# Masking attention probabilities by selection, and adding both key tiles on GpSimd before the row sums

## The reference

```
q = _l2norm(q) * q_scale;  k = _l2norm(k) * k_scale          # 16 heads of 64
sim = jnp.einsum('bhid,bhjd->bhij', q, k) * 8.0              # keys: 2 null keys and 256 rows
sim = sim + dist[None, None] * slopes[None, :, None, None]
sim = jnp.where(causal_mask[None, None], neg, sim)
attn = jax.nn.softmax(sim, axis=-1)
out = jnp.einsum('bhij,bhjd->bhid', attn, v)
```

## Time and profile before

| what | value |
|---|---|
| median of three runs | 976.25 us |
| the profiled execution | 976.13 us, of which 974.4 us are the span from first to last instruction |
| PE busy | 926.8 us (95%) |
| PEld, DVE busy | 708.9 us (73%), 736.5 us (76%) |
| ACT, POOL busy | 586.9 us (60%), 592.9 us (61%) |
| granted TensorE clock, mean | 0.989 |

### The profile page before, as it was taken

One profiled execution on the slowest core, in us unless ns is written; L12 is line 12 of the kernel. 1 busy time (PEld: TensorE's weight loads), 2 busy tenths in 40 slices (PEclk: granted clock), 3 DMA queues, 4 the chain that ended last, 5 costly groups with the idle time before them and its releaser, 6 DMA issues.

```text
span 974.4 us, 21588 instructions
## 1 busy us (share of the span) xinstructions
PE 926.8 (95%) x8309; PEld 708.9 (73%) x8309; DVE 736.5 (76%) x2334; ACT 586.9 (60%) x1235; POOL 592.9 (61%) x562
## 2 busy tenths in 40 slices
PE   1887999999999999999999999999999999999996
PEld 1575778687776878677786878668786878768755
DVE  6885578778788697868888787877977668864466
ACT  4448672867467662866648573775738574585622
POOL 5235773677547774677747875577744855458613
PEclk9979899999999999999999999999999999999999
DMA  5400000000000000000000000000000000000000
GB/s 156 109 0 11 2 3 2 0 12 2 13 1 12 1 2 13 1 11 2 13 1 1 12 2 13 1 11 2 12 2 1 1 1 13 1 1 2 13 1 12
DMA packets 22088, 11.50 MB, mean 12 GB/s; under 512 B 7648, under 2 KB 21344, under 8 KB 21856
## 3 DMA queue, kind: packets, MB, share of 16 engines
q1 hardware_dynamic: 20128, 9.51, 3.5%
q10 hardware_dynamic: 1856, 0.59, 0.2%
HBM read 8.00 MB, written 2.10 MB: 10 GB/s over the span
## 4 chain that ended last, share of the span: by engine, by line
PE 82%; DVE 8%; POOL 4%; ACT 4%; issue 1%; DMA 0%; DVEq 0%; ACTq 0%; POOLq 0%
PE bank L1987 8%; PE bank L1704 7%; PE bank L2024 6%; PE bank L1705 6%; PE bank L1706 6%; PE bank L1948 6%; PE bank L1985 5%; PE bank L1711 4%; PE bank L1857 4%; PE bank L1954 3%; PE bank L2120 3%; PE bank L2056 3%; PE bank L2126 3%; PE bank L2057 3%; POOL rnorm L920 3%; PE bank L1912 2%
## 5 line engine op out<-in xcount | busy, mean ns | idle before, releaser
L929 POOL TENSOR_TENSOR square<-square,causal 128x256 f32<-128x256 f32 x128 | 102.0, 821 | 54.4 <-ACT square L1169 54.4
L915 POOL TENSOR_TENSOR rnorm<-sumsq,minus_half 128x16 f32<-128x16 f32 x32 | 93.9, 2937 | 50.0 <-DVE sumsq L1526 49.8
L929 POOL TENSOR_TENSOR unit<-unit,causal 128x256 f32<-128x256 f32 x128 | 92.1, 745 | 38.3 <-ACT unit L1169 38.3
L1948 PE MATMUL bank<-qT,kT 64*128 64x256 f32 x512 | 95.2, 389 | 0.0
L920 POOL TENSOR_TENSOR rnorm<-unit,minus_half 128x32 f32<-128x32 f32 x16 | 91.4, 5720 | 0.0
L1163 ACT ACTIVATE square<-bank,bias_k,rnorm 128x256 f32<-128x256 f32 x128 | 65.7, 570 | 40.8 <-PE bank L1948 40.8
L1954 PE MATMUL bank<-qT,kT 64*128 64x128 f32 x512 | 84.0, 284 | 3.0 <-ACT unit L1169 2.2
L1954 PEld LDWEIGHTS bank<-qT,kT 64*128 64x128 f32 x512 | 71.0, 186 | 17.9 <-ACT unit L1169 6.7
L1948 PEld LDWEIGHTS bank<-qT,kT 64*128 64x128 f32 x512 | 68.7, 186 | 0.7
L1093 ACT ACTIVATE xaT_hi<-bank 128x256 fp32r<-128x256 f32 x16 | 5.5, 382 | 105.5 <-PE bank L1865 105.5
L1163 ACT ACTIVATE unit<-bank,bias_k,rnorm 128x256 f32<-128x256 f32 x96 | 51.4, 574 | 23.2 <-PE bank L1948 23.2
(11 more groups left out here) (402 smaller groups left out, 2905.8 us busy)
## 6 DMA issues: line engine op xcount, KB each, us to landing
xin<-in_L_attn_x SPq DMA_DIRECT2D x7, 256.0 KB, 2.8
out<-x SPq DMA_DIRECT2D x7, 256.0 KB, 2.3
square<-in_L_attn_w_kv SPq DMA_DIRECT2D x1, 1024.0 KB, 6.5
w_sw<-in_L_ffn_sw_w SPq DMA_DIRECT2D x3, 256.0 KB, 7.8
unit<-in_L_attn_w_q SPq DMA_DIRECT2D x1, 512.0 KB, 5.0
w_out<-in_L_attn_w_out SPq DMA_DIRECT2D x8, 64.0 KB, 2.1
w_ml<-in_L_ffn_ml_w SPq DMA_DIRECT2D x2, 256.0 KB, 6.0
xin<-in_L_attn_x ACTq DMA_DIRECT2D x1, 256.0 KB, 3.1
```

The lines of the kernel that those rows point to most:

```text
L915: pool.tensor_tensor(rnorm[:, 1, t, :], sumsq[:, t % 2, :], minus_half[:], ALU.pow).then_inc(a_root.sem, 1)
L929: m = pool.tensor_tensor(pd, pd, causal[:].unsqueeze(1).to_broadcast([P, 2, P]), ALU.mult)
L1948: return mm(bank[s][:, 2 * P * i:2 * P * (i + 1)], kT[rs, p, 2 * P * b:2 * P * b + P], qT[rs, p, 2 * P * b:2 * P * (b + 1)], start=True, s ...
```

## The change

1. Row sums. For the later queries POOL adds the probabilities of both key tiles (`late_sum`, 128x512 a unit, for four heads). PE then streams 128 columns of the sum, where it streamed 128 of key tile 1 and 128 of key tile 0. The weighted values are unchanged. A new semaphore `a_late` tells PE that the sum is there; PE waits for it between the two halves of the row sums.
2. Mask. The multiply by `causal` becomes an `affine_select` that writes zero where the key is later than the query. The six blocks of a pair of heads are laid out anew, so that the four blocks on the diagonal are contiguous: one instruction of 128x512 takes the place of two of 128x256. The tile `causal` and its set-up go.
3. Lists. The lists of all engines change in all stretches.

```diff
+        def early(pr, j):
+            return pr[:, 2 * j::4 - j, :]
+
+        def late(pr, j):
+            return pr[:, 2 * j + 1, :]
...
+        late_probs = []
+        for v in (unit_flat[:, 5 * N:5 * N + 2 * PH], square_flat[:, 0:2 * PH]):
+            blocks = v.rearrange("p (m i q) -> p m i q", m=2, q=P)
+            late_probs.append((blocks[:, :, 4:6, :], blocks[:, :, 1:4:2, :]))
+        late_sum = [hid_sw[1 + i].rearrange("p (m j q) -> p m j q", m=2, q=P) for i in range(2)]
...
                     pool.wait_ge(a_exp.sem, a_exp.at(g, 2 * h + 2))
-                    for b in range(SEQ):
-                        pd = probs[h % 4][:, b, 0::2, :]
-                        m = pool.tensor_tensor(pd, pd, causal[:].unsqueeze(1).to_broadcast([P, 2, P]), ALU.mult)
-                    m.then_inc(a_mask.sem, 1)
+                    pd = probs[h % 4][:, 0:4, :]
+                    pool.affine_select(out=pd, in_=pd, compare_op=ALU.is_ge, fill=0.0, base=0,
+                                       pattern=[[0, 4], [1, P]], channel_multiplier=-1).then_inc(a_mask.sem, 1)
+                pool.wait_ge(a_mask.sem, a_mask.at(g, 2 * c + 2))
+                if c > 1:
+                    pool.wait_ge(a_den.sem, a_den.at(g, c - 1))
+                elif first(g):
+                    pool.wait_ge(all_set, 1)
+                else:
+                    pool.wait_ge(f_e.sem, f_e.at(g - 1))
+                    pool.wait_ge(a_den.sem, a_den.at(g - 1))
+                pool.tensor_tensor(late_sum[c % 2], late_probs[c % 2][0], late_probs[c % 2][1], ALU.add).then_inc(a_late.sem, 1)
...
-                weigh(den, lambda k, h: ones[:]).then_inc(a_den.sem, 1)
+                for rs, h, pr, j in quad:
+                    mm(den[rs, 0:P], ones[:], early(pr, j)[:, 0, :], start=False, stop=True, skip_group_check=True)
+                pe.wait_ge(a_late.sem, a_late.at(g, c + 1))
+                for i, (rs, h, pr, j) in enumerate(quad):
+                    last = mm(den[rs, P:2 * P], ones[:], late_sum[c % 2][:, i % 2, j, :], start=False, stop=True, skip_group_check=True)
+                last.then_inc(a_den.sem, 1)
...
 MIDDLE = {
     "POOL": """
-a_keep f_stats.0 f_stats.1 a_ss.0 f_ce a_ss.1 a_ss.2 f_ce_apply f_ce2 a_ss.3 l_turn2 a_kss.0 l_res f_bias e_stats
+f_stats.0 f_stats.1 a_ss.0 f_ce a_ss.1 f_ce_apply a_ss.2 f_ce2 a_ss.3 l_turn2 l_res f_bias a_kss.0 a_kss.1 a_keep
```

More of the change, by code:

```diff
@@ L59 @@
     "PE": """
[L60 to L63, removed]
+a_m.0 a_m.1 a_k.0 a_null a_k.1 a_t.0 a_m.2 a_kr.0 a_k.2 a_k.3 a_t.1 a_kr.1 a_m.3 a_kt l_turn2 a_v.0 a_t.2 a_v.1
+a_t.3 l_turn3 a_v.2 l_route l_g.0 l_u.0 a_v.3 l_g.1 a_scores.0 l_u.1 l_cT a_nT l_g.2 a_scores.1 l_u.2 a_mix.0 l_c.0
+a_scores.2 a_mix.1 e_turn1 a_scores.3 l_g.3 a_mix.2 l_c.1 a_scores.4 l_u.3 l_g.4 a_mix.3 l_c.2 a_scores.5 a_mix.4
+l_c.3 a_scores.6 l_u.4 a_mix.5 a_scores.7 a_mix.6 l_down.0 l_down.1 a_mix.7 l_down.2 l_down.3 a_out.0 a_out.1 l_x.0
 l_x.1
@@ L549, in program @@
         a_mask = signal("a_mask", H)
+        a_late = signal("a_late", U)
         a_nT = signal("a_nT", 1)
@@ L1159, in score_exps @@
                         if h < STEEP:
-                            act.activation(pr[:, j, 0, :], k0[:, 0, :], ACT.Exp, bias=bias_k0[:, h:h + 1], scale=by)
-                            last = act.activation(pr[:, j, 1, :], k0[:, 1, :], ACT.Exp, bias=bias_k0b[:, h:h + 1], scale=by)
+                            act.activation(early(pr, j)[:, 0, :], k0[:, 0, :], ACT.Exp, bias=bias_k0[:, h:h + 1], scale=by)
+                            last = act.activation(early(pr, j)[:, 1, :], k0[:, 1, :], ACT.Exp, bias=bias_k0b[:, h:h + 1], scale=by)
                         else:
-                            last = act.activation(pr[:, j, 0:2, :], k0, ACT.Exp, bias=bias_k0[:, h:h + 1], scale=by)
+                            last = act.activation(early(pr, j), k0, ACT.Exp, bias=bias_k0[:, h:h + 1], scale=by)
                     last.then_inc(a_exp.sem, 1)
@@ L1168, in score_exps @@
                         by = rnorm[:, 0, 2 * b + 1, h:h + 1]
-                        last = act.activation(pr[:, j, 2, :], bank[2][:, 2 * P * s + P * j:2 * P * s + P * (j + 1)], ACT.Exp,
+                        last = act.activation(late(pr, j), bank[2][:, 2 * P * s + P * j:2 * P * s + P * (j + 1)], ACT.Exp,
                                               bias=bias_k1[:, h:h + 1], scale=by)
@@ L1980, in a_mix_ @@
                 b, q = unit_of(c)
-                quad = [(slice(32 * i, 32 * i + 32), QW * q + i, probs[(2 * c + i % 2) % 4][:, i // 2, :, :]) for i in range(QW)]
+                quad = [(slice(32 * i, 32 * i + 32), QW * q + i, probs[(2 * c + i % 2) % 4], i // 2) for i in range(QW)]
                 def weigh(dst, left):
-                    for rs, h, pr in quad:
-                        mm(dst[rs, P:2 * P], left(1, h), pr[:, 2, :], start=False, stop=False, skip_group_check=True)
-                    for rs, h, pr in quad:
-                        last = mm(dst[rs, :], left(0, h), pr[:, 0:2, :], start=False, stop=True, skip_group_check=True)
+                    for rs, h, pr, j in quad:
+                        mm(dst[rs, P:2 * P], left(1, h), late(pr, j), start=False, stop=False, skip_group_check=True)
+                    for rs, h, pr, j in quad:
+                        last = mm(dst[rs, :], left(0, h), early(pr, j), start=False, stop=True, skip_group_check=True)
                     return last
```

133 lines of the change are left out of this document (65 added, 68 removed).

## The result

| what | before | changed |
|---|---|---|
| median (runs) | 976.12 us (4) | 965.47 us (4; 965.29 to 968.65) |
| ratio to before, 95% interval | | 0.9896 [0.9881, 0.9911] |
| profiled execution, its span | 976.13 us, 974.4 us | 965.40 us, 963.7 us |

A forecast was written before the change was run, and what follows sets the result against it. PE was taken to bound the kernel, busy nearly all of each middle pass. Row sums 13.4 - last attention 1.3 - first attention 0.4 - moved steps 1.8 = 9.9 us; 976.13 - 9.9 = 966.2 us, range 961 to 972.5.

The forecast's parts named there:

- Row sums 0.67 to 0.46 us a unit: PE's row sums as two waves of 128 columns: 0.21 us saved a unit, 64 units, 13.4 us.
- the bound on the last attention: In the last attention ACT's exponentials set 4.55 us a unit, so units 0 to 5 lose their saving: 1.3 us.
- The new wait costs nothing for itself: PE's wait for POOL's sum between the row-sum halves: slack 0.4 us in tight units, so charged nothing.
- Select 0.60, add 1.27 us: POOL's 128x512 instructions: two selects and one add make 2.5 us a unit, 0.4 to 0.8 less than before.
- The bound of 2.6 us from L832: Upper bound for POOL's 128x512 select, if the 0.66 us of a 128x128 select were the rate for four blocks.
- Moved steps, 0.3 us a pass: Root behind the first sum, apply ahead of a_mix.0 delay unit 1's mixing: 1.8 us over five middle passes and the next.
- the 110.1 to 110.5 forecast: Sign of being right: a middle pass 110.1 to 110.5 us long, PE busy for nearly the whole of it.
- On DVE the other steps only change places in time that it has: DVE's list in the middle passes: 22 us idle a pass, so its other reordered steps cost nothing.
- set-up and tail at 0: Changed lists of the set-up and tail: taken as 0, with 1.5 us either way.
- The select may cost 1.0 before a tight unit waits: POOL's select, taken at 0.60 us, could reach 1.0 before PE waits for the sum in tight units; slack 0.4 us.
- The rival in which POOL becomes the bound: Select as slow as L832: sum late from 1.6 us each, 996 us at 2.0 us; chance 0.05.
- The rival of the wait, 972.2 us: The wait between PE's row-sum halves costs 0.1 us a unit, 6.4 us in all; chance 0.15, shared with a slower select.

The follow-up runs named there:

- e5: The kernel before, with a wait for a long-given semaphore (the mask's) between the two waves of its row sums: 976.04 us, ratio 0.9992.
- e11: The changed operations without the add, with the old lists; the late row sums stream the second key tile alone; against the kernel before: 965.26 us, ratio 0.9889.
- e12: The changed kernel (new lists) without the add, the late row sums streaming the second key tile alone: 964.85 us, ratio to the kernel before 0.9882.
- e2: The kernel before, its operations kept, with the changed kernel's work lists: 988.25 us, ratio 1.0127.
- e4: The kernel before with only the mask changed to one select of 128x512 a head pair, no add, old row sums and lists: 975.86 us.
- e10: The changed operations with the old lists and one POOL step moved, f_end_stats ahead of a_scores.5 in the middle passes: 965.95 us, ratio to before 0.9898.
- e3: The changed kernel with e_apply back behind a_mix.0 in DVE's list of the middle passes: 972.61 us, ratio to the kernel before 0.9969.
- e9: The changed kernel with the copy a_keep moved behind e_stats in POOL's list of the middle passes: 967.99 us, ratio to the kernel before 0.9914.
- e6: The changed kernel with each select made twice, a mask costing 1.3 us: 1009.33 us, ratio to the kernel before 1.0323.
- e8: The changed kernel with the mask by multiplication again, the add and short row sums kept: 1021.43 us, ratio to the kernel before 1.0454.

## Why the prediction was right, and where its terms were off

- **Row sums 0.67 to 0.46 us a unit.** Right (0.47 read), and so was the bound on the last attention: two units of eight keep their 0.21 us there, 0.42, and the stretch gave 0.41. The pass behind the middle ones gave 1.67 us = 8 x 0.21, so the 0.3 us that the prediction charged it was wrong.
- **The new wait costs nothing for itself.** Right: no idle time at it in the pass read, and e5 finds a granted wait free.
- **Select 0.60, add 1.27 us.** Right: median 0.64 and 1.27. The bound of 2.6 us from L832 was far off, and the trace of before could have told so. It has a second select of 128x128:

```profile
L794 POOL TENSOR_SCALAR_AFFINE_SELECT ident<-ident x1: 292/292/292, 1.6 to 1.6; 128x128 f32<-128x128 f32 x1
```

  It takes 0.29 us with DVE idle. L832 took 0.66 at 65.86, while DVE's L1304, which reads two tiles in SBUF, ran from 65.15 to 66.37. The figure in the Trainium skill ("GPSIMD Engine Reference", section "3. Performance versus the Vector engine"), 0.77 us for 512 elements by the best software loop, is too slow for this select.
- **Moved steps, 0.3 us a pass.** Right place and chain (root behind the sum, apply ahead of `a_mix.0`, unit 1's mixing), size half of what came: 0.63 us. The working had PE wait 0.1 us and rounded up to 0.3. Of the 0.5 us that this lacks, 0.31 are the apply, taken at 1.11 and measured at 1.42; the root ends 1.00 us behind the start of unit 0's mixing, where 0.73 was worked out. That a pass still came out at 110.33, inside the 110.1 to 110.5 forecast, needs 0.37 us of gain elsewhere (111.75 - 1.68 + 0.63 = 110.70 otherwise). e11 and e12 show that much and more as the gain of PE's new order, a term that the sum put at nothing. So the forecast's closeness is in part luck: two errors of the sum cancel here.
- **"On DVE the other steps only change places in time that it has", set-up and tail at 0.** The tail is right; the set-up can't be told. As a view of the lists it was wrong: alone they lose 12.7 us (e2). The 22 us of idle time a pass said nothing, since the loss comes from one chain that crosses from POOL to DVE.
- **"The select may cost 1.0 before a tight unit waits", and 996 us at 2.0.** This is the step that failed, though the forecast did not rest on it. At 1.3 us the kernel is at 1009 us, already slower than before, at 1.9 us at 1050. The slack of 0.4 us was computed for the sum alone, and the steps queued behind it on POOL, the roots for DVE and `e_scan`, were left out. It did no harm only because the select really took 0.64 us. The rival in which POOL becomes the bound was real and close: by a straight line between 0.64 us (965.5) and 1.3 us (1009.3) the changed kernel would be no faster than before from a select of 0.8 us on, not 1.6 (no run lies between), and its chance of 0.05 rested on the duration of one instruction that the trace did not show at this shape. The straight line is an estimate.
- **The rival of the wait, 972.2 us.** Its sum is off: 966.2 + 6.4 is 972.6. Nothing hangs on it.

What is shown: the gain is that of PE's columns (e11: 10.65 us without any add, against nothing in e4), less what the sum pushes back on POOL (0.56 to 0.67 us a pass), and the changed lists and one moved root (e10) each bring a like part back. Not tried: the new lists with the root `n_x_rstd` ahead of the first sum. e12's pass of 109.66 us bounds what that could bring at some 3 us.

## What to carry to other kernels

Slack belongs to an engine's whole list and not to one semaphore. When an in-order engine gets a new step, price everything queued behind it up to the next idle time, and what those outputs release on other engines. An operation that is worth nothing alone (the select: 0 us) can be what another one needs (56 us), so judge such changes together, and the order of the steps with them. Look for one step to move before writing new lists: in e10 one was enough. And compare the busy time of the bounding engine too, since its own order can be worth as much as an idle time (0.5 us a pass here).

## What the runs showed of the hardware

- **VectorE and GpSimd hold each other up, in these traces to the end of an instruction.** In the changed kernel the four applies of a pass (1.42 us from 556.35) begin just behind this select:

```profile
556.28 0.65 POOL L936 TENSOR_SCALAR_AFFINE_SELECT square<-square 128x512 f32<-128x512 f32 x1
```

  The first of them takes 0.65 us and ends 0.08 us after the select. With the sum in its place (e3) the four take 1.96 us, with four multiplies (e2) 2.81, with nothing beside them 1.11. A step of 0.17 us took 0.64 beside the copy (e9). The Trainium skill ("SBUF — State Buffer", section "Who interferes with whom") says that whoever of the two issues first gets the shared port pair for the whole instruction, and that `tensor_scalar` on VectorE can be such an instruction; the traces agree. So what POOL runs beside DVE's applies adds 0.3 to 1.7 us to them here. The prediction had asked what DVE does to the add, and not what POOL does to the applies.
- **Who starts first can hang on 0.02 us.** In the pass behind the middle ones a small step of DVE (L1494) takes 0.19 us in the changed kernel, where it starts with a select, which takes 0.69. In e9 the select starts 0.02 us before the step:

```profile
774.13 0.64 POOL L936 TENSOR_SCALAR_AFFINE_SELECT unit<-unit 128x512 f32<-128x512 f32 x1 [0.93 <-ACT unit L1185]
```

```profile
774.15 0.67 DVE L1494 TENSOR_TENSOR pick<-pick 128x32 f32<-128x32 f32 x1
```

  Now the select takes 0.64 us and the step 0.67, and the whole pass 0.47 us more (110.66 against 110.19). e12 has the same there (0.67 us, pass 110.62).
- **Select on GpSimd.** 128x512 in 0.63 us at the least and 0.64 in the median, up to 1.24 us beside a step of VectorE; 128x128 in 0.29 (once).
- **The granted clock makes the set-up's length differ between executions.** The changed kernel and e9 have the same lists up to the first scores, which start at 107.44 and 109.78 us. The windows of that stretch, changed kernel:

```profile
30.00:40.00 10.00, 9.09 (x48) 6.79 (x46) 7.73 (x24) 5.97 (x24) 8.05 (x21) 0.83 0.30 62
...
100.00:107.40 7.40, 7.40 (x37) 5.92 (x36) 4.28 (x28) 3.88 (x9) 7.40 (x2) 0.90 0.01 2
```

and e9:

```profile
30.00:40.00 10.00, 8.45 (x49) 6.15 (x48) 8.82 (x36) 6.75 (x25) 7.91 (x22) 1.00 0.34 77
...
100.00:107.40 7.40, 7.40 (x25) 6.27 (x24) 2.48 (x16) 1.59 (x4) 7.40 (x2) 0.50 0.01 2
```

  In the last of these stretches PE is busy throughout in both; at 0.50 it runs at the lower of its two levels, 1.2 GHz. Up to 97.4 us e9 was 1.4 us ahead; by the first scores it is 2.3 us behind. e12 was already 1.1 us behind the changed kernel by 34 us, at full clock, for a reason that stays open, so not all of its 3.5 us are the clock's. Over all kernels with these lists and at most one select a mask, the first cut lies between 161.6 and 165.1 us. e9's median stands 2.5 us above the changed kernel's with the same middle pass; in the traces it is 1.9 us, 1.52 up to the first cut and 0.47 in the pass behind the middle ones. The five middle passes of one trace agree to 0.05 us in nine of the fourteen kernels (0.07 in e11, 0.11 in e5, 1 us and more in e6 to e8), which is why differences of 1 to 3 us were read there.
- **PE can lose its clock in the middle too.** In e6 the same interval between two scores took 7.76 us in one pass and 10.72 in the next, where the clock was down for a part of it:

```profile
236.54:244.30 7.76, 5.31 (x80) 4.03 (x76) 7.46 (x15) 3.33 (x8) 7.34 (x10) 1.00 0.00 1
...
352.40:363.12 10.72, 8.28 (x80) 5.90 (x76) 7.93 (x15) 3.33 (x8) 7.82 (x10) 0.68 0.01 2
```

  In both PE was idle for 2.4 us of the interval, so the same idle time went once without and once with the lower clock. In the second PE's busy time is 3.0 us longer.
